# A hybrid network on one core: another order of the pieces on each engine, and another placing of the spare products

## The chip, the cores and the metric

The kernel runs on one core of one Trainium2 chip. A core has TensorE (PE in the profile), VectorE (DVE), ScalarE (ACT), GpSimd (POOL) and SyncE (SP), which issues DMAs. Each engine has its own stream of instructions and works through it in order; engines wait for each other through semaphores. The metric is device time of one execution in microseconds, lower is better.

## What is computed

2048 tokens of width 128 pass through eight residual stages. Each stage normalizes x and adds its result:

```python
x = x + _L0_attn_a_ref(_layernorm(x), ...)   # recurrence over the tokens, with clips
x = x + _L0_ffn_ref(_layernorm(x), ...)      # gated experts, two of eight
x = x + _L0_attn_b_ref(_layernorm(x), ...)   # picks 15 earlier tokens, small MLP, palette
x = x + _L0_ffn_ref(_layernorm(x), ...)
x = x + _L1_attn_a_ref(_layernorm(x), ...)   # linear attention, cumulative sums
x = x + _L1_ffn_ref(_layernorm(x), ...)
x = x + _L1_attn_b_ref(_layernorm(x), ...)   # attention with decay, a scan
x = x + _L1_ffn_ref(_layernorm(x), ...)
return x
```

The first is a chain over all tokens: `delta = clip(v_t - v_old)` needs the state that the token before left.

## The kernel before

The tokens are 16 tiles of 128. A tile goes through twelve stages, each with a letter: `f` front (norm, q, k, v), `g` gram, `s` scan (the recurrence), `o` out, `a` ffn2, `p` pal (logits, top 15), `m` mix (gathered rows, MLP, palette), `b` ffn4, `l` lin, `c` ffn6, `d` dec, `e` ffn8. Nearly every stage is causal, so tile i of a later stage needs only tiles up to i of the one ahead of it. While the scan works on tile 12, mix may work on tile 9 and ffn8 on tile 6.

Each engine's code of a stage is a generator that stops at a `yield` ahead of each piece. `ORDER` holds one string for each engine; a letter stands for the next piece of that stage. So the strings are the whole schedule: 2240 pieces on PE, 3856 on DVE, 1776 on ACT, 992 on POOL, 80 on SP. The function `fast` walks a string:

```python
for n, letter in enumerate(ORDER[engine]):
    before(n)
    next(runs[letter])
```

The scan takes 8 tokens as a block, 256 blocks in all. On DVE a block is four products (L949), four bounded scans (L957), a transpose (L929), a mask (L965) and an addition (L972). On PE it is two pieces of four small products each: L571 waits for the transpose on DVE, and L581 waits for the mask. L965 waits for L571 and L972 waits for L581. Every block therefore crosses between DVE and PE four times, and what stands ahead of L571 or L581 in PE's string is done before them. Gram (L557) prepares the coefficients. Lines of other stages that are named below: ffn2 and ffn4 L635 to L659, pal L671 to L687, mix L699 to L754, lin L765 to L784, ffn6 and ffn8 L795 to L826, dec L838 to L858; L529 is the transpose of every norm. The addition to x is L1165 on DVE for mix.

PE has four PSUM banks for all that is not scan state; `bank` gives them in turn, and waits until the last reader of the bank is done. `FILL` has a digit for each of PE's 2240 pieces: so many spare products stand ahead of the piece, in the bank that it takes. They write nothing that is read, and are there to keep PE at work:

```python
for _ in range(idle[0]):
    e.matmul(b[:, 0:512], identb[:, :], mup[:, 0:512], start=True, stop=True)
```

Of the kernel before, what the change touches and what calls it, by code (L numbers as in the profile page):

```python
# [92 lines left out]
def pieces(stage):  # L93

    for k, _ in enumerate(stage):
# [14 lines left out]
        "ssfffggfgsfsgssssfsssgsgsfsfssgsssssssgsssssssfssgsossosoosssofsgsfsososssasaasgssasaasasasassgspspsssspfssp"  # L110
        "ppopsgsosoosossfssfsgsososssaasasgssasaasasasassgsssmsmspsmfsmspsmmomgsmmmsosoomsospmssmppsmsmspspogsomsfsmm"
        "smmgsfssasaasssmmmmsmmamsaamsasasasmmsmsmsgpsomspfmsosomsososmgspssmmmpppmssmommmpogsmmssmsmssssmmmssmssssss"
        "sassgsaasofmsmsoomaasmmsaosasasaosmmmfsbgsbbspmsopmmmsbombbsmfbbbsmgsmpslslppppsmmmmsmmmmsagllslallslmmamlsl"
        "smsfgcasmcccccsmsamscscasmscasasaodfsdsmmmddsbmdbbommmsodpdddpmbobsbmombbbsmsmmsmlsmlsomsfspsmmmmmlllmslllop"
        "psppgmmfslflgmmscsgccccscsmcsmscssmasmcmsmsaaseseeeeemmmsdoseedasedddosoaooamddsmddasaasmmmsgsmmbmbsbmsopfmp"
        "osbmbmbsgbbsbmspgmspslppsmpmmmlsmamgasamllglllslmmsfamsaalmslfsamsascamcsccmmscccscbssbcbsopsepeeeeedsbseebd"
        "edddbsoombboddddsbosmmmmmsmmlsglssmmsmsomsllllllsommmsmsplslpsppmpmsamscfcmmmmmccccgasaccsmmcasmsaamedaseaem"
# [1944 lines left out]
```

## Time and profile before

| | us |
|---|---|
| median of three runs | 1591.43 |
| lowest and highest | 1584.05, 1592.32 |
| the profiled execution | 1597.4 |
| its span, first to last instruction | 1594.9 |
| PE busy (L517 of it) | 1352.4 (227.1) |
| DVE busy | 1066.4 |
| POOL busy | 906.0 |
| ACT busy | 843.5 |
| mean granted TensorE clock | 0.876 |

PE is the busiest engine, and a sixth of its busy time is spare products. A granted clock of 0.876 is a mean over stretches at 2.4 GHz and stretches at 1.2 GHz. Idle time of an engine costs something only where the chain that ends last passes through it.

### The profile page before, as it was taken

Reading aid. Unit: us, or ns where it says so; the run is one execution under the profiler, and the core shown is the slowest. Engines: PE = TensorE matmul, PEld = TensorE weight load, DVE = VectorE, ACT = ScalarE, POOL = GpSimd, SP = SyncE. Lnnn points to the kernel's source line nnn. Section 1 sums busy time; section 2 is a strip of 40 time slices with the busy share of each in tenths; the row PEclk is TensorE's granted clock in tenths of the full one; section 3 lists DMA queues with packets and bytes.
Section 4 is the critical chain, followed back from the end, with each engine's and each line's share of the span. In section 5 each row is a group of like instructions: output and inputs, shape, how many; then the busy total and the mean of one; then the engine's idle time right before and its main releaser. Section 6 shows DMA issues by size and latency. Waiting matters only on the chain.

```text
span 1594.9 us, 54156 instructions
## 1 busy us (share of the span) xinstructions
PE 1352.4 (85%) x21798; PEld 915.9 (57%) x21958; DVE 1066.4 (67%) x4616; ACT 843.5 (53%) x2254; POOL 906.0 (57%) x1527
## 2 busy tenths in 40 slices
PE   2668888888889898888899898899999899998886
PEld 1234555456567566656566565656666566765654
DVE  2787877878678867786866767586786746544332
ACT  1233254356475647474673746456464647565464
POOL 2545677567666847565766656465565456453331
PEclk8567668797989999988988899798899989999999
DMA  5000010000000101010100101000010101010000
GB/s 161 1 1 12 24 29 23 16 9 26 9 25 7 30 5 32 4 31 4 29 7 7 29 2 31 4 19 19 3 29 9 30 4 31 6 29 4 3 3 7
DMA packets 24294, 30.12 MB, mean 19 GB/s; under 512 B 9089, under 2 KB 18978, under 8 KB 24034
## 3 DMA queue, kind: packets, MB, share of 16 engines
q0 software_dynamic: 8304, 16.73, 4.1%
q1 hardware_dynamic: 15730, 9.82, 2.1%
q8 instruction: 176, 2.88, 0.8%
q14 instruction: 84, 0.69, 0.1%
HBM read 25.21 MB, written 2.29 MB: 17 GB/s over the span
## 4 chain that ended last, share of the span: by engine, by line
PE 54%; DVE 19%; ACT 11%; issue 8%; POOL 6%; SPq 1%; DMA 0%; DVEq 0%; ACTq 0%; POOLq 0%
PE ps L517 6%; PE ps L659 4%; PE ps L557 4%; DVE ps L957 4%; PE ps L754 3%; PE ps L712 3%; PE ps L742 2%; DVE ps L949 2%; PE ps L684 2%; PE ps L772 2%; PE ps L571 2%; POOL sb L1775 2%; PE ps L581 2%; PE ps L775 2%; PE ps L598 2%
## 5 line engine op out<-in xcount | busy, mean ns | idle before, releaser
L957 DVE TENSOR_TENSOR_SCAN ps<-ps,sb 128x47 f32<-128x47 f32 (+3 forms) x1024 | 272.0, 266 | 43.9 <-DVE ps L949 0.9
L1775 POOL DMA_INDIRECT sb<-table,sb x240 | 233.7, 974 | 92.9 <-issue 66.6
L517 PE MATMUL ps<-sb 128*128 128x512 bf16 x766 | 227.1, 396 | 17.1 <-issue 5.6
L949 DVE TENSOR_TENSOR ps<-sb,ps 128x24 f32<-128x24 f32 (+3 forms) x1024 | 192.9, 188 | 15.3
L517 PEld LDWEIGHTS ps<-sb 128*128 128x128 bf16 x926 | 86.5, 103 | 79.6 <-issue 20.9
L1639 POOL TENSOR_SCALAR sb<-sb 128x1 f32<-128x1 f32 x128 | 29.1, 227 | 170.5 <-DVE sb L892 164.6
L581 PEld LDWEIGHTS ps<-sb 32*32 32x32 f32 x2032 | 43.8, 112 | 123.3 <-issue 83.2
L571 PEld LDWEIGHTS ps<-sb 32*32 32x32 f32 x2032 | 43.6, 113 | 114.1 <-DVE sb L929 56.4
L898 DVE TENSOR_TENSOR sb<-ps,sb 128x128 f32<-128x128 f32 x112 | 31.8, 285 | 110.3 <-PE ps L826 57.8
L1289 ACT ACTIVATE sb<-sb 128x128 f32<-128x128 f32 x128 | 62.1, 489 | 81.6 <-POOL sb L1645 81.2
L571 PE MATMUL ps<-sb 32*32 32x32 f32 x2032 | 72.1, 214 | 36.4 <-DVE sb L929 33.8
L581 PE MATMUL ps<-sb 32*32 32x12 f32 x2032 | 66.1, 192 | 38.5 <-DVE sb L965 27.4
L557 PE MATMUL ps<-sb 128*128 128x480 f32 x128 | 85.7, 761 | 4.4 <-POOL sb L1678 2.3
L965 DVE TENSOR_TENSOR sb<-ps,sb 128x32 f32<-128x32 f32 x254 | 45.8, 180 | 57.8 <-PE ps L571 56.8
L1587 ACT ACTIVATE sb<-ps,sb 128x128 bf16<-128x128 f32 x256 | 71.1, 375 | 23.2 <-PE ps L816 23.0
L659 PE MATMUL ps<-sb 128*128 128x128 f32 x512 | 81.9, 312 | 0.0
L1678 POOL TENSOR_TENSOR sb<-sb 128x480 f32<-128x480 f32 x64 | 65.9, 1037 | 24.8 <-ACT sb L1333 24.7
L1643 POOL TENSOR_TENSOR sb<-sb 128x1 f32<-128x1 f32 x128 | 72.9, 569 | 10.8 <-POOL sb L1639 0.2
L972 DVE TENSOR_TENSOR ps<-sb,ps 128x12 f32<-128x12 f32 x254 | 41.0, 162 | 52.1 <-PE ps L581 51.0
L1817 POOL TENSOR_TENSOR sb<-sb 128x360 f32<-128x360 f32 (+1 forms) x48 | 48.7, 1017 | 46.2 <-ACT sb L1541 45.8
L1359 ACT ACTIVATE sb<-ps 128x480 f32<-128x480 f32 x64 | 37.0, 579 | 70.2 <-PE ps L557 68.7
L659 PEld LDWEIGHTS ps<-sb 128*128 128x128 f32 x512 | 73.6, 222 | 0.9
(310 smaller groups left out, 3777.0 us busy)
## 6 DMA issues: line engine op xcount, KB each, us to landing
sb<-table,sb POOLq DMA_INDIRECT x240
sb<-in_cs SPq DMA_DIRECT2D x16, 128.0 KB
table<-sb SPq DMA_DIRECT2D x17, 64.0 KB, 1.5
sb<-in_x SPq DMA_DIRECT2D x4, 256.0 KB, 8.0
sb<-dscr SPq DMA_DIRECT2D x64, 2.0 KB
out<-sb SPq DMA_DIRECT2D x16, 64.0 KB
sb<-in_mdn POOLq DMA_DIRECT2D x1, 512.0 KB, 9.9
sb<-in_wex SPq DMA_DIRECT2D x1, 512.0 KB, 7.4
```

The source lines that it names most:

```text
L517: e.matmul(b[:, 0:512], identb[:, :], mup[:, 0:512], start=True, stop=True)
L557: e.matmul(b[:, 0:32 * LW], blk, g_.pp[j % 2][:, :], start=True, stop=True).then_inc(*g_.P("s"))
L571: x = e.matmul(psS[rows, 0:32], KZT[c % 2][rows, 32 * o1:32 * o1 + 32], R[g % 2][rows, :], start=g == 0, stop=True, skip_group_check=True)
L581: x = e.matmul(b[rows, 0:12], SB[g % 2][rows, :], KM[c2 % 2][rows, 4 * o2:4 * o2 + 4, :].rearrange("p a b -> p (a b)"), start=True, stop=True)
L659: x = e.matmul(b[:, 0:128], s.hw[j // 4][:, 128 * (j % 4):128 * (j % 4) + 128], wex[:, 128 * j:128 * j + 128], start=False, stop=j == 7)
L949: e.tensor_tensor(at(psP, p + ROW - 3 - 2 * m, [ROW, 3], [2, m], [1, 2]), AC[:, row(n, k), :, HIST - 2 * m:HIST].rearrange("p r (a b) -> p ...
L957: e.tensor_tensor_scan(at(psD, 16 + k + COMB * skip, [COMB, 3 * ROW - skip]), at(psP, p + skip, [1, 3 * ROW - skip]), Q[:, i % 32, skip:3 ...
L1289: e.activation(s.xn[c % 2][:, :], X[:, s.tile(c), :], ACT.Identity, bias=st[:, 10:11], scale=st[:, 9:10]).then_inc(*s.A("xn"))
L1587: x = e.activation(s.w[:, 128 * at:128 * at + 128], bk.of[s.name, "d", g, c][:, 128 * j:128 * j + 128], ACT.Copy, scale=t[:, 40 + at:41 + at])
L1643: e.tensor_tensor(st[:, 9:10], st[:, 8:9], mhalf[:, 0:1], ALU.pow).then_inc(*s.G("lr"))
L1678: e.tensor_tensor(g_.pp[j % 2][:, :].rearrange("p (a b c) -> p a b c", b=2, c=LW), at(KT[c % 3], 32 * j, [2, 16], [0, 2], [1, LW]), km[:, ...
L1775: e.indirect_dma_start(GA[:, k, :], None, table[0:128 * i + 128, :] if i else table0, bass.IndirectOffsetOnAxis(u[:, k:k + 1], 0)).then_in ...
```

## The change

The five strings of `ORDER` are replaced and so is `FILL`; nothing else. Each engine has as many pieces of each stage as before, so no work of the network is added or taken away. By the digits in the code, the spare products are 1026 at 396 places, where they were 926 at 382. At the same place in the string another letter stands at 1658 of 2240 places on PE, 1350 of 3856 on DVE, 1240 of 1776 on ACT, 613 of 992 on POOL and 36 of 80 on SP. One line of PE's string and one of `FILL`:

```diff
-        "ppopsgsosoosossfssfsgsososssasaasgssasaasasasassgsssmsmspsmfsmspsmmomgsmmmsosoomsospmssmppsmsmspspogsomsfsmm"
+        "sppogsoossoossspsgssssososssasasasssasaasfasasasfgsmspsmspmsmsgospmfsmsosoopsompmmpmmmsmpmssmsgsmossosmmsmmf"
...
-    "0105000000010100000001010100000910002100000000100000000000100000010000010000000100100000000000000001000010000000"
+    "0010040007002403026034007010009021100200000101000400000000000200000130000000000000000006000100009000000107100000"
```

**Place 1: PE, about block 79 of 256 of the scan (the end of the scan's tile 4).** L571 and L581 are the scan's two pieces, L517 is a spare product. Before:

```order
L571 MATMUL ps<-sb 32x32 x4
L581 MATMUL ps<-sb 32x12 x4
L571 MATMUL ps<-sb 32x32 x4
L517 MATMUL ps<-sb 128x512 x3
L581 MATMUL ps<-sb 32x12 x4
L571 MATMUL ps<-sb 32x32 x4
L529 MATMUL ps<-sb 128x128
L517 MATMUL ps<-sb 128x512 x2
L581 MATMUL ps<-sb 32x12 x4
L571 MATMUL ps<-sb 32x32 x4
L517 MATMUL ps<-sb 128x512
```

Now:

```order
L571 MATMUL ps<-sb 32x32 x4
L635 MATMUL ps<-sb 128x8
L636 MATMUL ps<-sb 128x8
L640 MATMUL ps<-sb 128x128 x3
L641 MATMUL ps<-sb 128x128
L581 MATMUL ps<-sb 32x12 x4
L742 MATMUL ps<-sb 32x16 x80
L571 MATMUL ps<-sb 32x32 x4
L742 MATMUL ps<-sb 32x16 x16
L581 MATMUL ps<-sb 32x12 x4
L517 MATMUL ps<-sb 128x512 x2
L529 MATMUL ps<-sb 128x128
```

Where spare products alone stood between two steps of the scan, products of ffn2 and ffn4 (L640, L641) and of mix (L742) stand now. Over the whole of the scan's tile 4, PE has 104 pieces where it had 72.

**Place 2: PE, the end of mix for tile 11 (the last L754 of the tile).** Before:

```order
L754 MATMUL ps<-sb 32x128 x16
L614 MATMUL ps<-sb 128x128
L615 MATMUL ps<-sb 128x128
L571 MATMUL ps<-sb 32x32 x4
L754 MATMUL ps<-sb 32x128 x32
L529 MATMUL ps<-sb 128x128
L581 MATMUL ps<-sb 32x12 x4
L699 MATMUL ps<-sb 128x128 x4
L765 MATMUL ps<-sb 128x384
L571 MATMUL ps<-sb 32x32 x4
```

Now:

```order
L816 MATMUL ps<-sb 128x128
L815 MATMUL ps<-sb 128x128
L816 MATMUL ps<-sb 128x128
L754 MATMUL ps<-sb 32x128 x16
L815 MATMUL ps<-sb 128x128
L816 MATMUL ps<-sb 128x128
L815 MATMUL ps<-sb 128x128
L816 MATMUL ps<-sb 128x128
L815 MATMUL ps<-sb 128x128
```

The end of mix for tile 11 now stands 45 pieces nearer to the start of PE's string, and products of ffn6 and ffn8 (L815, L816) stand about it where steps of the scan and pieces of mix, pal and lin stood.

**Place 3: PE, behind the end of mix for tile 15, the last one.** L754 ends the tile's mix. Before:

```order
L754 MATMUL ps<-sb 32x128 x64
L772 MATMUL ps<-sb 128x360
L775 MATMUL ps<-sb 128x360
L858 MATMUL ps<-sb 128x128 x8
L772 MATMUL ps<-sb 128x360
L517 MATMUL ps<-sb 128x512
L529 MATMUL ps<-sb 128x128
L775 MATMUL ps<-sb 128x360
L635 MATMUL ps<-sb 128x8
```

Now:

```order
L754 MATMUL ps<-sb 32x128 x64
L529 MATMUL ps<-sb 128x128
L517 MATMUL ps<-sb 128x512 x2
L795 MATMUL ps<-sb 128x8
L798 MATMUL ps<-sb 128x128
L799 MATMUL ps<-sb 128x128
L807 MATMUL ps<-sb 128x128 x4
L517 MATMUL ps<-sb 128x512 x6
L529 MATMUL ps<-sb 128x128
```

Before, 92 pieces of PE stand behind that L754 and now 82; those of lin (L772, L775) and dec (L858) that followed it at once have gone ahead of it.

## Rows read from the trace of the kernel before

**Rows 1.** The page, part 1: busy time of each engine, share, instructions.

```profile
PE 1352.4 (85%) x21798; PEld 915.9 (57%) x21958; DVE 1066.4 (67%) x4616; ACT 843.5 (53%) x2254; POOL 906.0 (57%) x1527
```

**Rows 2.** The page, part 4: shares of the chain that ended last, by engine.

```profile
PE 54%; DVE 19%; ACT 11%; issue 8%; POOL 6%; SPq 1%; DMA 0%; DVEq 0%; ACTq 0%; POOLq 0%
PE ps L517 6%; PE ps L659 4%; PE ps L557 4%; DVE ps L957 4%; PE ps L754 3%; PE ps L712 3%; PE ps L742 2%; DVE ps L949 2%; PE ps L684 2%; PE ps L772 2%; PE ps L571 2%; POOL sb L1775 2%; PE ps L581 2%; PE ps L775 2%; PE ps L598 2%
```

**Rows 3.** Starts of L1165 (adds mix) and L957 (scan); the tile-11 L1165 in time order.

```profile
L1165 DVE SCALAR_TENSOR_TENSOR sb<-ps,sb x16: 319/349/352, 246.6 to 1499.3; 128x128 f32<-128x128 f32 x16
...
L957 DVE TENSOR_TENSOR_SCAN ps<-ps,sb x1024: 203/267/447, 45.0 to 1286.0; 128x47 f32<-128x47 f32 x86, 128x51 f32<-128x51 f32 x85
...
1220.03 0.35 DVE L1165 SCALAR_TENSOR_TENSOR sb<-ps,sb 128x128 f32<-128x128 f32 x1 [0.45 <-PE ps L754]
```

**Rows 4.** Stretches: PE, PEld, DVE, ACT, POOL busy (instructions), TensorE clock, DMA share, GB/s.

```profile
0.00:246.90 246.90, 167.38 (x2207) 95.44 (x2230) 170.38 (x883) 77.38 (x224) 129.87 (x253) 0.69 0.13 37
246.90:1220.40 973.50, 857.26 (x14652) 591.97 (x14754) 711.86 (x3154) 554.43 (x1477) 615.76 (x1026) 0.90 0.06 17
1220.40:1367.80 147.40, 134.84 (x2321) 94.99 (x2335) 94.32 (x324) 88.22 (x225) 79.00 (x117) 0.93 0.07 19
1367.80:1431.00 63.20, 59.17 (x1035) 41.03 (x1042) 29.94 (x75) 37.49 (x97) 31.94 (x49) 0.95 0.07 18
1431.00:1499.60 68.60, 58.87 (x1058) 43.58 (x1061) 27.17 (x71) 36.48 (x91) 25.34 (x39) 0.93 0.03 6
1499.60:1594.90 95.30, 74.87 (x532) 48.94 (x539) 32.70 (x112) 49.50 (x140) 24.12 (x46) 0.97 0.01 4
...
1306.50:1367.80 61.30, 57.53 (x1050) 42.16 (x1056) 33.94 (x91) 40.29 (x106) 36.85 (x55) 0.97 0.09 22
```

**Rows 5.** The same stretches, instructions of L517 (spare products) alone: PE, PEld.

```profile
0.00:246.90 246.90, 17.62 (x46) 6.73 (x68) 0.69 0.13 37
246.90:1220.40 973.50, 118.63 (x392) 45.35 (x495) 0.90 0.06 17
1220.40:1367.80 147.40, 26.61 (x97) 10.18 (x111) 0.93 0.07 19
1367.80:1431.00 63.20, 17.83 (x60) 6.78 (x67) 0.95 0.07 18
1431.00:1499.60 68.60, 12.12 (x41) 4.24 (x46) 0.93 0.03 6
1499.60:1594.90 95.30, 34.29 (x130) 13.26 (x139) 0.97 0.01 4
```

**Rows 6.** The page, part 5: groups of scan and gram on PE.

```profile
L571 PE MATMUL ps<-sb 32*32 32x32 f32 x2032 | 72.1, 214 | 36.4 <-DVE sb L929 33.8
L581 PE MATMUL ps<-sb 32*32 32x12 f32 x2032 | 66.1, 192 | 38.5 <-DVE sb L965 27.4
L557 PE MATMUL ps<-sb 128*128 128x480 f32 x128 | 85.7, 761 | 4.4 <-POOL sb L1678 2.3
```

**Rows 7.** Scan tile 4 and all behind the scan, each engine; then L517 there.

```profile
246.80:297.30 50.50, 38.70 (x701) 21.41 (x707) 38.48 (x207) 21.77 (x56) 36.40 (x53) 0.79 0.10 26
1286.00:1594.90 308.90, 269.91 (x4123) 190.09 (x4150) 134.91 (x375) 171.10 (x452) 129.60 (x206) 0.95 0.04 11
...
1286.00:1594.90 308.90, 76.71 (x278) 29.32 (x307) 0.95 0.04 11
```

**Rows 8.** Two stretches with their clock, then L659 on PE in each.

```profile
173.50:193.50 20.00, 17.40 (x211) 12.26 (x212) 15.77 (x86) 5.31 (x18) 10.27 (x18) 0.50 0.06 18
471.00:555.00 84.00, 76.26 (x1277) 52.83 (x1284) 67.33 (x302) 49.88 (x139) 56.88 (x97) 1.00 0.07 17
...
L659 PE MATMUL ps<-sb x12: 421/421/582, 175.8 to 178.8; 128*128 128x128 f32 x12
...
L659 PE MATMUL ps<-sb x32: 274/275/378, 501.2 to 533.6; 128*128 128x128 f32 x32
```

**Rows 9.** The last chain, from 1499 us on: its summary line.

```profile
by line: issue 22.2%; ACT sb L1575 4.6%; ACT sb L1579 4.5%; PE ps L517 4.0%; PE ps L850 3.2%; DVE sb L1223 3.1%; POOL sb L1643 3.0%; PE ps L775 2.7%; ACT sb L1587 2.3%; PE ps L772 2.1%; POOL sb L1842 2.0%; ACT sb L1289 2.0%; PE ps L659 1.9%
```

More of the change, by code:

```diff
@@ new lines @@
+        "smmsmmslsopslopspmmsmmgllllllsmmaspaammlglsmsmfmcmascpcccsmmmmaccsacsascsaasfseeeeesemsmmdemsesmdedsddbmbbmm"
+        "spdgdddmmmsbpombsboosbsbbososglfsslssmlllosllslommmspglspslmmmspmmammmascaccccpscpgmsccscmssmmsammedsmaemeee"
+        "sedefaedddsaaaesfdmmsdddsmmmmmpsmgsbmsbbsmmmosfbpsoosboogsbsmbbsbsmmmssolpslsmmmosppslllllslmamamammsppggsfl"
+        "mslmmmscfsmmmamcsccccsaassccaascsgsammmmmmesmmeeeeesdmmesmsmdesdbsddebbsoddsfdpdsobobboosbsbbpsgmmmlsmslomsm"
+        "mspmospplllmmmsmlllsappmsagasmllmsmfgmmsmmscfcccccsascscaascasaasseeeemmemsmesedesmpdmbmesddbpdbgmsgsdddsodm"
@@ new lines @@
+        "daaagsddsddasaaosmsmbsobbsooospmbmsbpbmmmsbbbsosmopmsmmmlpsplsmsmsallllllsmmasalsmmslmmppcsccccsccccsseeeeee"
+        "daeesmdsemsaddmmmmdmmasmddaaasdmsdmmsbmbbpmssommpobobmbmobbbompmmmmmlplmmoplllolllmmpplmmlaaammcccccccccaeaa"
+        "deedmeemmdmdmmmmdaaammeemmddeddbebbpmmpmmbbbmmmpbbbppmmmmbpblblmpmmllllllbbbmbbbmlmmlmmlclcccccllllccllcleld"
+        "eeedmmdeddemmmmemmeddeddmmmcmccmmmbmbbmmccmmmcmmmbcbbcmbbbcmmmldlmdmemmdddlleeleeldddeldlemmmmemmmmlelmmmmcc"
+        "ccbccbbcccbbbeeeebbbeedelldedddlllllleldldddcccccccccedeedededdeeeddeddeeeeeeeee",
@@ new lines @@
+    "POOL":
+        "ffffggfggggfffggggffgggggffggggoofgoooooooffggapggppppfpggoogppppooooooopppappppppfggppgpfgfppppfoopggfooooo"
+        "ppooppppappmmppppppmpfgfggpggfpppoogpoooooooggpagfpppppppppppmbmpppmppfgffggpglpppoollllollloooooocgpaggfgpp"
+        "ppppppdppppgpppddddmmgfmbpgffggoogggooofloopooplllpllpllapgggcgppppppppppedppppgmmpmddddbpgffooppfppoooooolo"
+        "ggpfllllalllppppcpppppppppmmppedmgpbgggfffddddgooppppolooooollollglglflagpggcpppppppppppdegppppmgmddmddpfbfg"
+        "fooppppfoooooologggpllllallplpppppcgpppppfgmmppppmedbgpggffddddoofoooolopppoopgllplllalglggpppppcpppmmpppppp"
+        "edmbpfpffgggddddoopppgpooooloogopllllalllggcpppppppmpmpepdppmppppbggfddddggppooppgooolfoooopllllallflfggcggp"
+        "pppppppppmmppedmpppbpfgggddddppppoooloooooolflllplallffgcgggfpppppppedppggppppmmppgmddddggbpoooooooooppplfpa"
+        "fpflllllllggggcgmmmedggppppppppppppdddpdppbooggpoooopopoopplpalllllllcmmmppedppppppppppddpddppbpooppppopoloo"
+        "ooolllllllacppppppmmpedmppppppddddbppppppppblllllllplpppppplcpmpllllppllmledmppppddddcbldellmmlddddlmlllcbed"
+        "lllllldlldddceddddde",
@@ L197 @@
     "SP":
[L198 removed]
+        "ppppmpppmpppmppmpppmppepppemppmpeeppmppmpppppeempmpppemeppppmpepmeppeppmppmeeeee",
 }
 FILL = (
[L201 to L203 removed]
```

186 lines of the change are left out of this document (82 added, 104 removed).

## The prediction, made before the changed kernel ran

> **What bounds the kernel now.** I read the busy times first. PE is busy for 1352.4 of 1594.9 us, DVE for 67%, the others for less [rows 1]. The chain that ended last lies on PE for 54% and on DVE for 19% [rows 2]. So no engine is full, and PE's stream is what most work queues in. Next I cut the execution where mix of a tile ends (L1165), because mix has the most work per tile; it ends first at 246.6 us, for tile 11 at 1220.4 and for tile 15 at 1499.6 [rows 3]. For each stretch I read PE's busy time [rows 4] and take off the spare products [rows 5]. The reader is to see three parts:
>
> - 0 to 246.9 us: PE has 167.4 - 17.6 = 149.8 us of real work and 79.5 us of idle time, at a granted clock of 0.69. The pipeline of tiles fills here.
> - 246.9 to 1220.4: 857.3 - 118.6 = 738.6 us of real work in 973.5 us, so 1.318 us pass for each us of real work. 116.2 us are idle. The clock is 0.90.
> - Behind it: 1220.4 to 1367.8 has 108.2 us of real work in 147.4 (a ratio of 1.362), the stretch to 1431.0 has 41.3 in 63.2, the one to 1499.6 has 46.8 in 68.6, and the last has 40.6 in 95.3. The scan is over at 1286.0 [rows 3].
>
> The last stretch is another kind: 22% of its chain is issue, and ACT, DVE and POOL lines follow each other in it [rows 9]. There the last tile's own path decides, not the amount of work on PE.
>
> **The change.** Nothing is added but 100 spare products, and the other pieces are the same in number. So the question is where PE's work stands relative to the things that end the stretches. I count letters of PE's two strings up to each end of a mix tile. The price of a piece comes from the trace: a scan piece costs (72.1 + 66.1) / 512 = 0.27 us, a gram piece 85.7 / 64 = 1.34 us [rows 6], and any other (1352.4 - 227.1 - 138.2 - 85.7) / 1664 = 0.54 us [rows 1, 5, 6]. A spare product costs 227.1 / 926 = 0.245 us of PE, the sums of the busy time and of the weight loads of L517 [rows 5].
>
> Step 1, up to the end of mix 11 (place 2): 45 pieces fewer, namely 10 of scan, 1 of gram and 34 others. That is -2.7 - 1.3 - 18.4 = -22.4 us of real work. By the ratio 1.318 it gives -29.5 us. DVE's string agrees in direction (that L1165 stands 85 pieces earlier), and so do ACT's (32) and POOL's (20), so I see no engine that would keep PE waiting for what has been drawn ahead.
>
> Step 2, mix 12 and 13: most of it comes back. Mix 12 has 7 scan pieces, 1 gram piece and 19 others more (+13.5 us), mix 13 has 3 scan pieces and 7 others more (+4.6 us). At 1.362 that is +24.7 us.
>
> Step 3, mix 14: 26 other pieces more, +14.1 us. The ratio would be 1.53 here, but 17.8 us of the stretch are spare products, and their number falls from 67 to 49. I therefore add up: 41.3 + 14.1 of work, 49 x 0.245 = 12.0 of spare products, 4.0 of idle time as before, 71.4 us. That is +8.2.
>
> Step 4, mix 15: 8 other pieces fewer (-4.3), spare products 18 for 47. The sum would be 42.5 + 4.4 + 9.7 = 56.6 us. The shortest distance between two ends of mix in the tail is 61.3 us (tile 13, from 1306.5 to 1367.8) [rows 4], and mix has its own path of gathered rows, MLP and palette, so I take 61.3: -7.3 us.
>
> Step 5, behind mix 15 (place 3): 10 pieces fewer (-5.4) and 101 spare products for 139 (-9.3). All of it on the path would be -14.7; none, 0. As the row of the last chain shows issue and other engines rather than PE, I take -5.
>
> Step 6, the spare products ahead of mix 11: 734 for 563. Of these, 64 more stand ahead of mix 0, where 79.5 us of PE are idle: they cost nothing there, and 15.7 us at most if that cover were gone. The other 107 come to 26.2 us beside 116.2 us of idle time. L517 has about 6% of the chain [rows 2], 94 us of its 227, or 0.41. By that share they cost 10.7 us; the ends are 0 and 26.2. Against it stands the clock. A 128x128 float32 product of L659 takes 421 ns where the granted clock is 0.50 (1.2 GHz) and 275 ns where it is 1.00 (2.4 GHz) [rows 8], 35% less. One hundredth more of granted clock over 973.5 us is 19.5 us less at 1.2 GHz; with 54% of the chain on PE that is 19.5 x 0.54 x 0.35 = 3.7 us. More spare products between the pieces may bring 0 to 0.06. I take 0.03, -11.1 us, and let the two cancel.
>
> The Trainium skill (TensorE: Matmul & The Clock Gate, section Terms) prices throttled time at the time times (1 - K/N), one half. By that the 0.03 would be 29 us and not 11, and the sum some 18 us lower. The trace speaks against it for this mix of work: the product above loses 35% and not 50%, and only part of the time has PE on the chain.
>
> **Place 1, the one that speaks against the change.** In the scan's tile 4 PE has 72 pieces and is busy for 38.7 of 50.5 us, at least 6 us of it spare products [rows 7]. It gets 32 pieces more: 2 front, 8 ffn2, 9 ffn4 and 14 mix, less 1 gram: 33 x 0.54 - 1.34 = +16.5 us. These come to about 49 us of real work in a stretch of 50.5, so L571 and L581 will be behind them and the scan must slow down here, by 10 to 20 us. What is queued behind it on DVE are the four products and scans of each block. I cost it at nothing more than step 1 counts, because later stages have a backlog of two tiles and get their work done in that time. It costs if the scan's end decides (below).
>
> **The sum:** -29.5 + 24.7 + 8.2 - 7.3 - 5 + 0 = -8.9 us. The profiled execution took 1597.4 us (its span is 1594.9), so it would be 1588.5. The median of the three runs is 1591.43, 0.99626 of the profiled one; by that the forecast is 1582.6 us.
>
> **Rivals.**
>
> *The spare products do not fit (slower).* On PE they run ahead of the piece for which they stand, and if that piece's inputs are there, everything behind it is late. Then the work moved ahead of mix 11 brings its bare 22.4 us and not 29.5, and the 107 cost their whole 26.2: +3.8 in place of -29.5, so +24.4 in all. 1621.8, or 1615.7 on the median's scale. It decides from about a third of the 107 on the path beyond the share taken. For it speaks that L517 is on the chain for more time than any other line [rows 2]; against it, the 116 us of idle time.
>
> *The scan's end decides (no change).* On PE the scan's last piece stands 23 pieces later: 14 mix, 6 dec, 2 ffn4, 1 pal, 12.5 us, x 1.318 = +16.4 us. What follows is the last tile's path, 308.9 us, of which PE is busy for 269.9 and 76.7 are spare products [rows 7]. If only the work that moved is saved there (12.5), the result is +3.9: 1601.3, or 1595.3. For it speaks place 1, and that this stretch has 210 spare products for 310 only because less idle time is there to fill; against it, that mix's backlog hides a late scan.
>
> *The clock (clearly faster).* The spare products fit, cost nothing, and raise the clock of the long stretch by 0.06: -22.2 beside -8.9. 1566.3, or 1560.4. For it: the clock is at 0.69 in the first stretch and 0.90 in the long one [rows 4], with 79.5 and 116.2 us of idle time to fill. Against it: in the first stretches DVE's scan sets the pace, which a faster PE helps little. By the skill's rule named above this case would be still lower; I have not used that.
>
> **Chances.** The forecast 0.40, the clock 0.24, spare products that don't fit 0.19, the scan's end 0.14, anything else 0.03. A measurement of this kernel can tell about 0.5%, 8 us, from no change. The forecast is just beyond that, so I split its 0.40 into 0.22 faster, 0.15 the same, 0.03 slower. The clock gives 0.24 faster; the spare products 0.19 slower; the scan's end 0.11 the same and 0.03 slower; the rest 0.01 the same and 0.02 slower. In sum 0.46 faster, 0.27 the same, 0.27 slower. The range reaches from the clock's case with a little more (1556) to the spare products' case (1618). The likeliest case alone, with the ends of steps 5 and 6, spans 1568 to 1603.
>
> **What would show it.** Step 1: the L1165 of tile 11 at about 1191 us and not 1220. Steps 2 and 3: mix 13 ends 5 us earlier than before (about 1363) and mix 14 some 3 us later (1434). Step 4: 61 us from mix 14 to mix 15. Step 5: about 90 us from there to the end. Step 6: a granted clock of about 0.93 in the long stretch, with L517 at about 0.4 of its busy time on the chain. Place 1: the scan's tile 4 takes 60 to 70 us and not 50, and the scan ends 10 to 20 us later than 1286. The forecast is wrong if mix 11 does not end earlier, or if idle time on PE in the long stretch stays near 116 us although the spare products are more.

## The result, and the profile after

The changed kernel takes 1546.18 us in the median of four runs (1541.74 to 1548.0), beside 1588.37 us for the kernel before on the same chips. The ratio is 0.972, with a 95% interval from 0.966 to 0.977. The forecast was 1582.6 us, with a range down to 1556: the sign was right, the size was missed by a factor of five, and the time lies below the range. The profiled execution took 1547.8 us where that of before took 1597.4, so 49.6 us have to be found in the traces; by the medians it is 42 us, because the profiled execution of before was slower than all the timed ones (1592.32 at most).

The page after: busy times, spare products, the chain that ended last by engine and by line.

```profile
PE 1360.1 (88%) x22058; PEld 893.6 (58%) x22058; DVE 1056.4 (68%) x4616; ACT 840.2 (54%) x2253; POOL 909.9 (59%) x1527
...
PE 60%; DVE 14%; ACT 8%; POOL 8%; issue 7%; SPq 1%; DMA 0%; DVEq 0%; POOLq 0%; ACTq 0%
PE ps L517 9%; PE ps L659 4%; PE ps L557 4%; PE ps L754 4%; PE ps L712 3%; PE ps L742 2%; DVE ps L957 2%; PE ps L571 2%; POOL sb L1775 2%; PE ps L581 2%; PE ps L598 2%; PE ps L684 2%; DVE sb L1223 2%; PE ps L772 2%; PE ps L601 2%
...
L517 PE MATMUL ps<-sb 128*128 128x512 bf16 x1026 | 304.2, 399 | 7.6 <-ACT sb L1575 1.7
```

Against [rows 1] and [rows 2]: PE is busy for 88% of the span and not 85%, and 60% of the chain lie on it and not 54%. L517 has 9% of the chain where it had 6%. So the spare products hold more of the path than in the page of before (which lacks some of them, see below), and the kernel is faster nonetheless. The granted clock is 0.914 for 0.876.

There is also a thing about [rows 1] that I had in front of me and did not use. There PE shows 21798 products to 21958 weight loads. After shows 22058 to 22058. The trace of before lacks 160 records, all of L517: 766 products in its page (a sum of 227.1 us) to the 926 weight loads of [rows 5]. A spare product is 304.2 / 1026 = 0.30 us of PE, and 227.1 / 766 is the same. My 0.245 divided the time of 766 by 926. The missing ones also read as idle time of PE: at the weight loads of the 103 that the long stretch lacks, the trace of before shows gaps of about 12 us in all, so I estimate the 116.2 us of idle time in the prediction at 104.

The same cuts as in [rows 4] and [rows 5], at the ends of mix 0, 11, 13, 14 and 15 (stretch; PE, PEld, DVE, ACT, POOL busy; clock; DMA), then L517 alone.

```profile
0.00:252.10 252.10, 177.26 (x2319) 96.27 (x2319) 174.35 (x900) 77.41 (x228) 132.46 (x258) 0.76 0.13 37
252.10:1160.80 908.70, 843.56 (x14620) 557.85 (x14621) 672.90 (x3034) 542.41 (x1439) 587.22 (x975) 0.94 0.06 17
1160.80:1329.40 168.60, 156.16 (x2524) 107.86 (x2522) 114.59 (x413) 94.26 (x246) 105.69 (x162) 0.96 0.08 20
1329.40:1408.30 78.90, 69.59 (x1135) 50.22 (x1134) 41.47 (x105) 46.00 (x124) 45.09 (x67) 0.98 0.08 20
1408.30:1461.90 53.60, 48.17 (x993) 37.20 (x992) 22.86 (x67) 32.42 (x82) 18.82 (x29) 0.88 0.01 4
1461.90:1546.00 84.10, 65.32 (x476) 44.21 (x474) 30.22 (x102) 47.69 (x136) 20.59 (x39) 0.93 0.02 4
...
0.00:252.10 252.10, 40.83 (x131) 11.50 (x131) 0.76 0.13 37
252.10:1160.80 908.70, 179.29 (x604) 53.66 (x604) 0.94 0.06 17
1160.80:1329.40 168.60, 35.98 (x124) 11.24 (x123) 0.96 0.08 20
1329.40:1408.30 78.90, 13.51 (x49) 4.39 (x49) 0.98 0.08 20
1408.30:1461.90 53.60, 5.68 (x19) 1.99 (x20) 0.88 0.01 4
1461.90:1546.00 84.10, 28.87 (x101) 9.27 (x99) 0.93 0.02 4
```

Beside [rows 4] the six stretches changed by +5.2, -64.8, +21.2, +15.7, -15.0 and -11.2 us. The pattern of the forecast is there: early at mix 11, given back up to mix 14, gained again behind it. Step 2 was foreseen within 4 us (+21.2 for +24.7); all others are larger than forecast. PE is idle for 65.1 us of the long stretch.

Start and end of mix's additions and of the scan, for [rows 3]; and the scan's tile 4 (place 1), for [rows 7].

```profile
L1165 DVE SCALAR_TENSOR_TENSOR sb<-ps,sb x16: 325/351/352, 251.8 to 1461.5; 128x128 f32<-128x128 f32 x16
...
L957 DVE TENSOR_TENSOR_SCAN ps<-ps,sb x1024: 200/267/445, 44.8 to 1261.9; 128x47 f32<-128x47 f32 x86, 128x51 f32<-128x51 f32 x85
...
247.70:311.30 63.60, 56.77 (x1247) 39.02 (x1243) 47.97 (x250) 30.30 (x79) 43.88 (x75) 0.89 0.08 22
```

The scan's tile 4 takes 63.6 us for 50.5, as its 32 further pieces on PE led me to expect. But the scan ends at 1261.9 and not later than 1286.0.

### The profile page after: what moved, and what is told of

Read it like the earlier page. It is cut to its first block, busy times and chain, and to the rows that moved or that the text cites. A ratio compares the mean times of both kernels' runs of the same rounds, so it can differ in the third digit from the quotient of the medians.

```text
span 1546.0 us, 54480 instructions
## 1 busy us (share of the span) xinstructions
PE 1360.1 (88%) x22058; PEld 893.6 (58%) x22058; DVE 1056.4 (68%) x4616; ACT 840.2 (54%) x2253; POOL 909.9 (59%) x1527
## 4 chain that ended last, share of the span: by engine, by line
PE 60%; DVE 14%; ACT 8%; POOL 8%; issue 7%; SPq 1%; DMA 0%; DVEq 0%; POOLq 0%; ACTq 0%
PE ps L517 9%; PE ps L659 4%; PE ps L557 4%; PE ps L754 4%; PE ps L712 3%; PE ps L742 2%; DVE ps L957 2%; PE ps L571 2%; POOL sb L1775 2%; PE ps L581 2%; PE ps L598 2%; PE ps L684 2%; DVE sb L1223 2%; PE ps L772 2%; PE ps L601 2%
## 5 line engine op out<-in xcount | busy, mean ns | idle before, releaser
L517 PE MATMUL ps<-sb 128*128 128x512 bf16 x1026 | 304.2, 399 | 7.6 <-ACT sb L1575 1.7
L957 DVE TENSOR_TENSOR_SCAN ps<-ps,sb 128x47 f32<-128x47 f32 (+3 forms) x1024 | 272.1, 266 | 42.7
L517 PEld LDWEIGHTS ps<-sb 128*128 128x128 bf16 x1026 | 92.1, 102 | 87.6 <-issue 23.1
L581 PEld LDWEIGHTS ps<-sb 32*32 32x32 f32 x2032 | 42.2, 109 | 104.8 <-issue 69.3
L571 PEld LDWEIGHTS ps<-sb 32*32 32x32 f32 x2032 | 42.0, 109 | 100.8 <-DVE sb L929 48.8
L571 PE MATMUL ps<-sb 32*32 32x32 f32 x2032 | 70.0, 209 | 24.3 <-DVE sb L929 23.8
L557 PE MATMUL ps<-sb 128*128 128x480 f32 x128 | 81.1, 726 | 2.9 <-POOL sb L1678 2.4
L581 PE MATMUL ps<-sb 32*32 32x12 f32 x2032 | 64.8, 189 | 18.1 <-DVE sb L965 13.4
L1643 POOL TENSOR_TENSOR sb<-sb 128x1 f32<-128x1 f32 x128 | 72.6, 568 | 10.7 <-POOL sb L1639 0.2
L659 PE MATMUL ps<-sb 128*128 128x128 f32 x512 | 76.1, 299 | 0.0
L754 PE MATMUL ps<-sb 16*32 16x128 f32 x2048 | 71.4, 290 | 0.0
L659 PEld LDWEIGHTS ps<-sb 128*128 128x128 f32 x512 | 68.9, 210 | 2.2 <-issue 1.4
```

The source lines that it names most:

```text
L557: e.matmul(b[:, 0:32 * LW], blk, g_.pp[j % 2][:, :], start=True, stop=True).then_inc(*g_.P("s"))
L571: x = e.matmul(psS[rows, 0:32], KZT[c % 2][rows, 32 * o1:32 * o1 + 32], R[g % 2][rows, :], start=g == 0, stop=True, skip_group_check=True)
L581: x = e.matmul(b[rows, 0:12], SB[g % 2][rows, :], KM[c2 % 2][rows, 4 * o2:4 * o2 + 4, :].rearrange("p a b -> p (a b)"), start=True, stop=True)
L659: x = e.matmul(b[:, 0:128], s.hw[j // 4][:, 128 * (j % 4):128 * (j % 4) + 128], wex[:, 128 * j:128 * j + 128], start=False, stop=j == 7)
L754: x = e.matmul(b[32 * q:32 * q + 32, 0:128], WT[rows, k:512:16], palW[rows, 128 * k:128 * k + 128], start=k == 0, stop=k == 15)
L957: e.tensor_tensor_scan(at(psD, 16 + k + COMB * skip, [COMB, 3 * ROW - skip]), at(psP, p + skip, [1, 3 * ROW - skip]), Q[:, i % 32, skip:3 ...
```

## The experiments

All ratios are to the kernel before, timed on the same chip in turn with it. Intervals are 95%.

| kernel | order | spare products | ratio | interval | clock in the profile |
|---|---|---|---|---|---|
| before | before | 926 | 1 | | 0.876 |
| after | after | 1026 | 0.972 | 0.966 to 0.977 | 0.914 |
| bo_none | before | 0 | 1.015 | 1.006 to 1.025 | 0.783 |
| ao_none | after | 0 | 1.001 | 0.997 to 1.006 | 0.791 |
| bo_afill | before | after's 1026, by piece | 1.051 | 1.042 to 1.061 | 0.883 |
| ao_bfill | after | before's 926, by piece | 1.030 | 1.021 to 1.040 | 0.876 |
| spB_11_none | before, after's behind mix 11 | 0 | 1.004 | 1.000 to 1.008 | 0.785 |
| spA_12_none | after, before's behind mix 12 | 0 | 1.012 | 1.006 to 1.018 | 0.786 |
| af_front | after | 734 ahead of mix 11's end | 0.979 | 0.972 to 0.987 | 0.891 |
| af_back | after | 292 behind it | 0.991 | 0.987 to 0.995 | 0.818 |
| bf_front | before | 563 ahead of it | 1.007 | 1.003 to 1.011 | 0.801 |
| bf_back | before | 363 behind it | 0.994 | 0.991 to 0.997 | 0.787 |
| after_b | after | 1026 | 0.972 | 0.968 to 0.976 | 0.924 |
| af_gap_b | after | 603, placed by a trace | 0.978 | 0.973 to 0.984 | 0.874 |
| af_trim_b | after | 435 of 1026 | 0.986 | 0.983 to 0.990 | 0.851 |
| bf_gap | before | 614, placed by a trace | 0.980 | 0.975 to 0.985 | 0.884 |
| af_more | after | 1282 | 0.970 | 0.964 to 0.976 | 0.951 |
| af_gap2 | after | 692, two turns | 0.967 | 0.962 to 0.972 | 0.901 |

In the last column is the clock of one execution. A ratio compares a kernel with before on one chip; the kernels ran on five chips, in the groups bo_none to ao_bfill; the two spliced ones (spB, spA) with af_front and af_back; bf_front and bf_back; after_b to bf_gap; af_more and af_gap2. So a ratio of one group beside one of another carries the uncertainty of both.

af_trim and af_gap ran first on the chip of bf_front and bf_back, on which before took 1748 us, 10% more than elsewhere (0.976 and 0.967 there, clocks 0.809 and 0.829). On another chip the same two kernels came to 0.986 and 0.978, 1.0 and 1.2 points higher. bf_front and bf_back ran only on the slow chip, and a ratio from there can be off by as much.

### Order and spare products apart

My theory: the order makes the gain, and the spare products cancel. The rival: the spare products and the clock make it. Four kernels part them. Two have no spare products (the old lines are cut short here):

```diff
 FILL = (
-    "0000...",
+    "0" * 2240)
```

> The order of before with no spare products at all. It gives the base for the order alone, and says what the 926 spare products of before bring. If the order of the pieces makes the gain, the order of after without spare products is 2 to 3% faster than this kernel. If the spare products (the clock) make it, the two are within 0.5% of each other. For this kernel by itself: the granted clock falls from 0.88 to about 0.75, and the time rises by 2 to 5% over before, unless the 926 cost on PE what they give back in clock, when it is within 1%.

> The order of after with no spare products. Order theory: 0.97 to 0.98 of the order of before without spare products. Clock theory: 0.995 to 1.005 of it, at nearly the same clock of about 0.75.

Two have the other kernel's spare products, carried to the same pieces. One line of FILL, of bo_afill against before and of ao_bfill against after:

```diff
-    "1000010000100000000000000000100200000000100003000000000500000020000200100200000000000000010003000000000000000000"
+    "2200000000010000000000600000010000200000003020000001000000093000120000000000000010000210200000012000010000000000"
```

```diff
-    "0022040026000100000000000010000000020000000000010000000009301003000200000000001001200000100000200000200000000001"
+    "0010000000000000010000001501002000000010000000300000001200000000200000020000000000000100000000000000000000000000"
```

> The order of before, with the spare products of after: each of the 396 places goes with its piece (the k-th piece of its stage), so 1026 spare products stand ahead of the same pieces as in after. Clock theory (it is number and kind of place that count): 0.975 to 0.985 of before, at a clock of about 0.91. Order theory: 0.995 to 1.005 of before. A third theory, that spare products fit only the order for which they were placed, gives 1.005 to 1.02.

> The order of after, with the 926 spare products of before carried to the same pieces. Order theory: 0.97 to 0.98 of before. Clock theory: 0.995 to 1.005 of before, at a clock of about 0.88. The third theory (spare products fit only their own order): between the two, 0.98 to 1.0, with more L517 on the chain than after's 9%.

Measured: 1.015 and 1.001 without any, 1.051 and 1.030 with the other's. Without spare products the order is worth 1.001 / 1.015, or 1.4%. That is between the two theories (2 to 3%, and under 0.5%), so neither holds alone. The forecast had 0.55%. For bo_none by itself I had expected a clock of about 0.75 and 2 to 5% more time; it is 0.783 and 1.5%. The spare products bring 1.5% to before and 3.0% to after, from 1.001 to 0.972; so half of the result is theirs. At the other order's pieces some thousand of them cost 2.9% and 3.6% against none at all, although the clock (0.876 and 0.883) is far above the 0.78 without any. Of the three theories in the expectations the third, that they fit only the order for which they were placed, is nearest for both, and both came out slower than even it expected (1.051 for 1.005 to 1.02, 1.030 for 0.98 to 1.0). So neither their number nor the clock that they keep up decides, but where they stand. A count fits with this: in the traces without spare products, 377 of before's own 926 and 429 of after's own 1026 stand at a piece ahead of which PE is idle for over 0.1 us (41% and 42%); of those carried over it is 254 of 1026 in bo_afill (25%) and 187 of 926 in ao_bfill (20%). The first rival of the forecast was this mechanism, and it is real; only the change itself did not suffer from it.

The stretches of bo_none and then of ao_none, cut at the ends of mix 0, 11, 13, 14 and 15:

```profile
0.00:246.90 246.90, 157.66 (x2162) 92.55 (x2163) 170.95 (x887) 77.37 (x224) 130.66 (x254) 0.66 0.14 37
246.90:1230.60 983.70, 831.88 (x14260) 593.83 (x14258) 709.66 (x3148) 554.55 (x1477) 614.07 (x1024) 0.81 0.06 16
1230.60:1374.30 143.70, 121.34 (x2223) 89.95 (x2223) 94.84 (x325) 87.36 (x225) 79.11 (x117) 0.85 0.08 19
1374.30:1437.40 63.10, 54.65 (x975) 40.34 (x975) 29.79 (x77) 37.31 (x97) 31.94 (x49) 0.80 0.07 18
1437.40:1508.90 71.50, 58.70 (x1017) 45.42 (x1015) 27.20 (x71) 36.38 (x91) 25.52 (x40) 0.80 0.02 6
1508.90:1612.90 104.00, 65.31 (x403) 51.79 (x401) 32.89 (x112) 50.27 (x140) 23.91 (x45) 0.69 0.01 3
...
0.00:250.90 250.90, 154.96 (x2188) 91.80 (x2188) 175.79 (x900) 77.35 (x228) 132.26 (x258) 0.66 0.13 37
250.90:1175.60 924.70, 800.87 (x14014) 566.57 (x14014) 668.48 (x3034) 541.98 (x1439) 589.97 (x977) 0.82 0.06 17
1175.60:1351.30 175.70, 145.70 (x2402) 110.33 (x2401) 114.58 (x413) 95.02 (x246) 103.50 (x160) 0.83 0.07 19
1351.30:1434.70 83.40, 69.29 (x1086) 53.30 (x1086) 41.28 (x106) 46.32 (x124) 45.03 (x67) 0.82 0.07 19
1434.70:1486.60 51.90, 44.66 (x974) 35.47 (x973) 22.77 (x67) 32.14 (x82) 18.79 (x29) 0.89 0.02 4
1486.60:1576.90 90.30, 58.30 (x375) 48.63 (x375) 30.17 (x103) 48.59 (x136) 20.56 (x39) 0.67 0.01 4
```

The order alone changes them by +4.0, -59.0, +32.0, +20.3, -19.6 and -13.7 us, together -36.0. By the medians it is -24 (1614.5 and 1590.5): the profiled execution of ao_none was 12 us faster than its median, so single stretches here are good to some us only. The real work on PE up to the end of mix 11 falls from 157.7 + 831.9 = 989.6 us to 155.0 + 800.9 = 955.9. That is -33.7 for the 45 pieces, at nearly the same clock in both, and the forecast had -22.4.

### Where in the order the gain is

I believed that the gain is made by mix 11. Two kernels cut the strings in two, on all five engines, and carry on in the other's order. Of PE's string, spB_11_none against before, the line with the seam:

```diff
-        "mebddbbdooosodddsdbmpbmbmpmbbbsmsomosmmlsmlsmmspmsllsllsllspppspmmlsmmmlmmmasaammcmccscccmssccmmmmscsasaasee"
+        "mebddbbdooosodddsdbmpbmbmpmbbbsmsomosmmmmmmmmmsssmpmsmmmlpsplsmsmsallllllsmmasalsmmslmmppcsccccsccccsseeeeee"
```

> No spare products. All engines follow the order of before up to the end of mix 11 (PE's first 1767 pieces and what they need on the others), and then the order of after for what is left. If the order's gain is made ahead of mix 11 and partly given back behind it (in the two kernels without spare products the end of mix 11 was at 1230.6 and 1175.6 us and what followed took 382 and 401 us), this kernel has neither and is slower than both: about 1632 us in the profile. If the gain lies in the tail's order, it is at about 1590.

The line of spA_12_none with its seam, against after:

```diff
-        "daeesmdsemsaddmmmmdmmasmddaaasdmsdmmsbmbbpmssommpobobmbmobbbompmmmmmlplmmoplllolllmmpplmmlaaammcccccccccaeaa"
+        "daeesmdsemsaddmmmmdmmasmddaaasdmsdmmbsssbbpoooboobbbbbplolommmmllllllpmmmppppmmmmalmalammmcmccccmmmmccccaaaa"
```

> No spare products. All engines follow the order of after up to the end of mix 12, and then the order of before for what is left. By the same sum, after's way to mix 12 (1275.7 us) and before's behind it (302.6 us): about 1578 us in the profile, as the order of after itself (1576.9). If the gain lies in the tail's order, 1595 or more.

Measured: before's order with after's tail is at 1.004, just 0.3 points from after's order (1.001) and 1.1 from its own (1.015). After's order with before's tail is at 1.012. Both pairs say that the tail is worth 1.1 of the 1.4 points and the long front about 0.3. The front's part is smaller than the intervals and may be nothing; spliced and unspliced kernels ran on different chips, but the two ways to the tail's 1.1 agree. For the first my expectation of about 1632 us (1603 in its profile) was wrong by nearly 30 us, and for the second that of 1578 by 21; the alternative that I had named for each, that the gain lies in the tail's order, came closer. After's order ends mix 12 at 1277.3 us in spA_12_none, 33 us ahead of bo_none (1310.4), and with before's tail 13 us of that are left at the end of the span (1599.5 to 1612.9). Even these come from one fast execution: by the medians spA_12_none is 0.3 points ahead of bo_none. Pieces that are put off until after a milestone make the milestone earlier and are paid behind it; its earlier date is no gain.

Behind the end of mix 15 the part of the tail can be seen by itself. The last stretch of bo_none and ao_none stands above, with 104.0 and 90.4 us. That of spB_11_none (after's tail) and then of spA_12_none (before's tail):

```profile
1511.00:1601.40 90.40, 58.68 (x375) 48.49 (x375) 29.96 (x103) 48.74 (x136) 20.58 (x39) 0.67 0.01 4
...
1495.50:1599.50 104.00, 65.02 (x403) 51.67 (x401) 32.93 (x112) 50.34 (x140) 24.13 (x45) 0.69 0.01 3
```

90.4 and 104.0: in these four traces it goes with the tail's order. On PE 375 products stand there in after's tail and 403 in before's. Step 5 of the forecast had this part with the value -5, of which the 10 pieces could give -5.4 at most (the rest of its bound of -14.7 was spare products); here, without any spare products, it is -13.6.

### Where the spare products gain

Two kernels have a part of after's spare products each. af_front keeps those ahead of the end of mix 11, af_back those behind. One line of FILL, of the part that is set to zero in each:

```diff
-    "3000020100000000000000010002300609049100100000000000000000000000000000000000000001200000000000000000000003010000"
+    "0000000000000000000000000000000000000000000000000000000000000000000000000000000000000000000000000000000000000000"
```

```diff
-    "0022040026000100000000000010000000020000000000010000000009301003000200000000001001200000100000200000200000000001"
+    "0000000000000000000000000000000000000000000000000000000000000000000000000000000000000000000000000000000000000000"
```

> The order of after with its own spare products, but those behind the end of mix 11 left out (734 of 1026 stay). The spare products of after bring 2.8% over the same order without any. If the long stretches ahead of mix 11 carry that (idle time there and a clock of 0.82 without them), this kernel keeps three quarters of it: about 0.979 to 0.984 of before.

> The order of after with only the 292 spare products behind the end of mix 11. If the gain goes by the share of the time, this one keeps a quarter: 0.990 to 0.997 of before. If the tail, where the last tile's own path decides, gains most from the clock (0.67 in the last 90 us without spare products), it keeps half or more, 0.98 to 0.988.

The same for the order of before:

```diff
-    "0000000000000010402170000551000013200307000000000004000000000000030000000001011000000010000000000000030000000000"
+    "0000000000000000000000000000000000000000000000000000000000000000000000000000000000000000000000000000000000000000"
```

```diff
-    "1000010000100000000000000000100200000000100003000000000500000020000200100200000000000000010003000000000000000000"
+    "0000000000000000000000000000000000000000000000000000000000000000000000000000000000000000000000000000000000000000"
```

> The order of before with its 563 spare products ahead of the end of mix 11, and none behind it. All 926 bring 1.5% here. Ahead of mix 11, after's 734 brought 2.2 points. If it is the front where after's placing is the better one, this kernel is at 1.005 to 1.015 of before (it keeps 0 to 1 point of the 1.5). If it is the back, it keeps 1.5 or more: 0.99 to 1.0.

> The order of before with only its 363 spare products behind the end of mix 11. If the front's are the poor ones, this keeps 1 point or more of the 1.5: 0.998 to 1.006 of before. If the back's are, 1.01 to 1.02.

In after, the 734 of the front bring 1.9 points (0.991 to 0.972) and the 292 of the tail 0.7 (0.979 to 0.972). Alone, without the others, they bring 2.2 and 1.0 (from 1.001). In before the 363 of the tail bring as much, 0.7 (1.007 to 1). But the 563 of the front cost 0.6: without them before is at 0.994. That is where I had expected the poor ones, though bf_back, at 0.994, lies below both ranges that I gave for it. So my reading was that before's spare products did harm in the front.

That is not shown. The last two numbers come from the slow chip, where the two kernels that were timed elsewhere too had ratios lower by 1.0 and 1.2 points, more than the 0.6 in question. And the traces from the other chips show no harm: mix 11 ends at 1220.4 us with before's spare products and at 1230.6 without any (after: 1160.8 and 1175.6), while on the slow chip it ends at 1363.8 with the 563 (bf_front) and at 1343.2 without them (bf_back). What is shown is the whole, 1.5% for before's and 3.0% for after's.

### Are spare products free where the trace shows PE idle?

For the count above I matched PE's instructions in the traces without spare products to the pieces of the string, and took the idle time ahead of each piece. Ahead of mix 11's end 192 of before's 563 spare products stand at a place with over 0.1 us of it, and 280 of after's 734; behind it 185 of 363 and 149 of 292. The tails are alike in this too, half and half; in the front 34% and 38% are too close to explain the difference by this count alone. af_trim keeps 435 of after's spare products, those at a place with over 0.1 us of idle time in that trace or with some left behind them in after's own. af_gap drops all places and takes new ones: at each piece that takes a bank and has over 0.3 us of idle time ahead of it, as many as fit at 0.25 us. Lines of FILL against after:

```diff
-    "0022040026000100000000000010000000020000000000010000000009301003000200000000001001200000100000200000200000000001"
+    "0000040026000000000000000010000000000000000000000000000000000003000000000000000000000000000000000000200000000000"
```

```diff
-    "0022040026000100000000000010000000020000000000010000000009301003000200000000001001200000100000200000200000000001"
+    "0000012012200000000000000030000000000000000000000500000000070002000000000000000000000040000000000000000000000000"
```

> The order of after, with 435 of its 1026 spare products: those at places where the trace of the order without spare products shows PE idle for over 0.1 us before the piece, or where the trace of after shows idle time left behind them. If a spare product is free only in a gap that the trace shows, the 591 that are left out only cost, and this is faster than after: 0.955 to 0.968 of before. If they pay through the clock wherever they stand, it loses some of it: 0.980 to 0.990.

> The order of after, with 603 spare products at 204 new places: wherever the trace of this order without spare products shows PE idle for over 0.3 us before a piece that takes a bank, as many as fit at 0.25 us each. If gaps in one trace say where spare products are free, this is as good as after or better: 0.960 to 0.975 of before. If the gaps of one execution aren't where those of the next are, it costs: 0.99 to 1.02, as the carried ones did.

On the slow chip: 0.976 and 0.967. So that they could be set beside after, both ran again on one chip with it, and with the same rule on the order of before:

```diff
-    "1000010000100000000000000000100200000000100003000000000500000020000200100200000000000000010003000000000000000000"
+    "0000010000000000000000000001000100000000000000000002000000000210000000000200000000000000000005001000000000000000"
```

> The changed kernel again, on one chip with the three below, so that they can be compared with it directly: 0.965 to 0.977 of before.

> The order of after with 603 spare products at the 204 places where the trace without spare products shows PE idle for over 0.3 us. In the last comparison it was at 0.967 of before, on a chip on which every kernel took 10% longer. If that holds here it equals after (0.965 to 0.977) with 423 spare products fewer, and number and clock don't matter as much as place. If it came from that chip's longer idle times, 0.98 to 0.99 here.

> 435 of after's spare products, those at places with idle time. 0.976 of before in the last comparison. If the 591 left out are neither cost nor gain: as after. If they pay through the clock: 0.5 to 1 point slower than after.

> The order of before with spare products placed by the same rule as in af_gap, from the trace of its own order without any. If before's own 926 are placed poorly and the rule is good, this takes the order of before to 0.980 to 0.990 of before, and what is left to after is the order's own 1.4 points. If before's order has less room for spare products wherever they stand, it is 0.995 or more.

Measured: 0.972, 0.978, 0.986 and 0.980. af_gap_b falls just behind the range for "equals after" (0.965 to 0.977), and af_trim_b lost 1.4 points where I had expected 0.5 to 1. The last is the one that tells most. The order of before, with 614 spare products at other places in place of 926, is 2.0% faster than before. Its clock; from its page the lines on busy time and chain, the chain's lines and its spare products; and its long stretch:

```profile
core 0: 1568.6 us, clock 0.884
...
PE 1337.2 (85%) x21646; PEld 880.1 (56%) x21646; DVE 1063.7 (68%) x4616; ACT 842.1 (54%) x2254; POOL 908.0 (58%) x1527
...
PE 49%; DVE 22%; ACT 12%; issue 8%; POOL 7%; SPq 1%; DMA 0%; DVEq 0%; ACTq 0%; POOLq 0%
DVE ps L957 4%; PE ps L517 4%; PE ps L754 4%; PE ps L659 4%; PE ps L557 3%; PE ps L712 3%; DVE ps L949 3%; POOL sb L1775 3%; PE ps L684 2%; PE ps L742 2%; PE ps L772 2%; PE ps L571 2%; PE ps L775 2%; PE ps L581 2%; PE ps L850 1%
...
L517 PE MATMUL ps<-sb 128*128 128x512 bf16 x614 | 193.9, 430 | 51.7 <-DVE ps L972 8.2
...
247.10:1204.50 957.40, 838.42 (x14557) 565.31 (x14556) 709.79 (x3154) 554.44 (x1477) 615.50 (x1025) 0.90 0.06 17
```

The clock is 0.884, and before had 0.878 to 0.889 on that chip: the same. L517 has 4% of the chain for 6%. The end of mix 11 is at 1204.5 us, 16 earlier than in [rows 4], with the same 0.90 of clock in the long stretch. So another placing, with a third fewer spare products, gives the 2.0% at an equal clock. Fewer at the old places was not tried in this order; in after's (af_trim_b) it cost time. With spare products placed by the same rule the two orders are at 0.978 and 0.980, alike within their intervals: the 1.4 points that the order has without spare products are not seen any more.

But the trace of the order without spare products does not say it all. The 591 that af_trim drops stand where that trace shows no gap of 0.1 us, and they are worth 1.4 points (0.986 to 0.972). Two things could make it: with the spare products in, PE waits elsewhere than in that trace; or they pay through the clock (0.851 in af_trim_b, 0.924 in after_b). These runs don't part the two.

### More of them, and a better version

af_more adds 256 to after's, where two traces of after still show idle time. af_gap2 applies the rule a second time, on the trace of af_gap_b, and adds 89.

```diff
-    "0022040026000100000000000010000000020000000000010000000009301003000200000000001001200000100000200000200000000001"
+    "0022040026000100000000000040000000020000000000010600000009301003000200000000001001200040100000200000200000000001"
```

```diff
-    "0022040026000100000000000010000000020000000000010000000009301003000200000000001001200000100000200000200000000001"
+    "0000012012200000000000000050000000000000000000000500000000070002000000000000000000050040000000000000000000000000"
```

> After with 256 spare products more (1282), put where two traces of after both still show PE idle for over 0.3 us before a piece that takes a bank. If what is free can be read from the idle time, it is faster than after: 0.960 to 0.970 of before, at a clock of 0.93. If the little that is left is eaten by spare products that hold up PE, it is 0.972 to 0.985.

> The order of after with the spare products placed by its trace without any (603), and 89 more where the trace of that kernel still shows idle time over 0.3 us. A second turn of the rule: 0.970 to 0.978 of before if each turn finds free places, as af_gap (0.978) if it doesn't.

Measured: 0.970 and 0.967. Page lines of af_more, then of af_gap2 (clock; chain by engine; spare products):

```profile
core 0: 1542.0 us, clock 0.951
...
PE 59%; DVE 15%; ACT 10%; POOL 7%; issue 7%; SPq 1%; DMA 0%; DVEq 0%; POOLq 0%; ACTq 0%
...
L517 PE MATMUL ps<-sb 128*128 128x512 bf16 x1282 | 372.3, 395 | 27.0 <-DVE sb L1165 4.8
```

```profile
core 0: 1532.3 us, clock 0.901
...
PE 45%; DVE 18%; ACT 12%; POOL 12%; issue 10%; SPq 1%; DMA 0%; DVEq 0%; POOLq 0%; ACTq 0%
...
L517 PE MATMUL ps<-sb 128*128 128x512 bf16 x692 | 220.7, 432 | 45.5 <-DVE sb L1165 5.3
```

I expected 0.960 to 0.970 for af_more and 0.970 to 0.978 for af_gap2. af_more has the highest clock of all, 0.951, and 59% of its chain on PE; it is not clearly faster than after. af_gap2 has 692 spare products, a clock of 0.901 and 45% of the chain on PE, and it is the fastest kernel of the study, at 1543.3 us to 1598.6 for before on its chip. Its interval (0.962 to 0.972) and after's (0.966 to 0.977) overlap, so with two thirds of the spare products it is as good as after as far as these runs tell; that it is better is likely and not shown. Whether the order of before would get there too after a second turn was not tried.

## Why the prediction was wrong, point by point

**Which step failed.** Step 6 put the spare products at nothing, and they are half of the result; beside it steps 4 and 5 had the tail too small. The forecast for all up to the end of mix 14 was +3.4 us (steps 1 to 3, with 0 for step 6). The traces show -22.7 from before to after, and -2.7 between the two orders without spare products. So the moving of work was nearly the exchange that the forecast said, and the missing 20 us came in with the spare products. (These are single executions, and the one of ao_none was 12 us faster than its median.) For the two stretches behind mix 14 the forecast was -12.3 us; the traces show -26.2, and -33.3 without spare products.

**What bounds the kernel.** That no engine is full, that the fill, the long stretch and the tail have different limits, and that the last stretch hangs on the last tile's own path: no run speaks against it.

**Step 1** (end of mix 11 about 29 us earlier): it is 60 us earlier, 1160.8 for 1220.4, and 55 without spare products. The mechanism was right and the price too low. The 0.54 us for a piece came from PE's busy time less all of L517's. L517's time overlaps that of the products next to it, and taking it off took real work with it: in the trace of before the products other than L517 keep PE busy for 1192.1 us, not 1125.3. In bo_none, where none stand and the clock is lower, it is 1289.5 us. The earlier date was given back in steps 2 and 3, and the spliced orders show the same: the work is only moved. The forecast had that; my expectation of 1632 us for the first of them left it out.

**Steps 2 and 3** (+24.7 and +8.2, together +32.9): +36.9 in after, +52.3 without spare products. Right in kind; step 3 was low (+15.7 for +8.2).

**Step 4** (-7.3): -15.0. The shortest distance of two mix ends, 61.3 us, was taken for a floor. It is none: here it is 53.6 us, and 51.9 without spare products. A smallest value among four is no bound.

**Step 5** (-5, bounds 0 and -14.7): -11.2 in after, -13.7 and -13.6 in the two comparisons without spare products. I had allowed the 10 pieces -5.4 at most; the path got shorter by more than twice that. PE's busy time there fell by 7.0 us (65.3 to 58.3), and what the rest is was not looked into. This is the part of the order's gain that the experiments pin down best.

**Step 6** (0) is the step that failed, and it is half of the result. I let 10.7 us of cost and 11.1 us of clock cancel for *more* spare products. The question was not the 100 more but where all 1026 stand. The runs showed that all of before's bring 1.5% and all of after's 3.0%, so the new ones are worth 1.5 points more in their order than the old ones in theirs, some 24 us. bf_gap gains 2.0% in the order of before by another placing, at the clock of before. The forecast had no term for how well before's were placed. The clock of the long stretch rose from 0.90 to 0.94, between the forecast's 0.93 and the third rival's 0.96; by the 3.7 us for a hundredth it would give 15 us. The cost was too low in turn: at 0.30 us each, the 107 are 32 us and not 26.2. L517 was to be on the chain for 0.4 of its busy time; it is 9% of 1546.0 us, 139 of 304, or 0.46.

**The clock's price.** A granted clock of 0.876 is 24.8% of 1594.9 us at 1.2 GHz, and 0.914 is 17.2% of 1546.0: 130 us less. All that was gained is 49.6 us, by the ratios half of it the order's, and af_more, with 0.951, gained no more. The Trainium skill (TensorE: Matmul & The Clock Gate, section Terms) prices throttled time at the time times one half, which would be 65 us. The runs don't agree with it as a price of the whole time in this kernel; what the spare products cost in PE's time is in the measured number too and was not measured apart.

**The rivals.** The clock's case was nearest, at 1560.4, and still short by 14 us. Spare products that don't fit: the mechanism is real (2.9 and 3.6% when carried to the other order), and the change doesn't have it. The scan's end: tile 4 slowed as said, 63.6 us, and then the scan ended 24 us earlier; PE was no longer held up as often elsewhere. That last is argued, not shown.

**The range.** Its lower end was the clock's case with a little more, and it had no room for a gain by place. The narrower span of 1568 to 1603 mixes two scales: its lower end is in time of the profiled execution, and on the median's scale it is 1562.

**What stays open:** how the order's 1.4 points vanish once both orders have spare products placed by the same rule, whether the changed order as such is needed for 0.967, and in which stretches before's spare products stood badly.

## What to carry to other kernels

A milestone that comes earlier because work was moved behind it is not yet a gain; splice the two orders at the milestone and see what the end says. When instructions exist only to keep a clock up, ask of each whether its engine waits at that very place, and read it from a trace: 614 at places read from one beat 926 by 2%. And check that a trace has all records of a line (here products against weight loads) before dividing its time by a count.

## What the runs showed of the hardware that was not expected

One chip of the five on which the experiments ran took longer: 10% for before, 9% for af_gap and af_trim, the other kernels that ran there and elsewhere. The same kernel (af_gap and af_gap_b), the groups of two lines with very many small products, on the slow chip and then on another:

```profile
L742 PE MATMUL ps<-sb 15*32 15x16 f32 x4096 | 62.6, 191 | 34.9 <-issue 34.6 <-POOL sb L1794 0.3
L734 PE MATMUL ps<-sb 128*32 128x3 f32 x1920 | 49.2, 204 | 32.8 <-issue 31.5 <-ACT sb L1496 1.1
```

```profile
L742 PE MATMUL ps<-sb 15*32 15x16 f32 x4096 | 52.8, 187 | 17.7 <-issue 16.2 <-POOL sb L1794 1.4
L734 PE MATMUL ps<-sb 128*32 128x3 f32 x1920 | 37.6, 204 | 2.6 <-issue 1.5 <-ACT sb L1496 1.1
```

The mean product is as long on both (191 and 187 ns, 204 and 204), but PE stands idle ahead of L734 for 32.8 us and not 2.6, with no wait that the profile shows for most of it, and the span is 1707.6 us for 1559.6. L734's busy time is longer too (49.2 for 37.6 us), although each product is not, so they follow one another with less overlap. Busy and idle time of the two lines together make 69 of the 148 us; the clock is lower as well, 0.829 for 0.874. What makes the small products follow more slowly, and where the rest of the time goes, was not looked into.

The granted clock and the time do not go together across these kernels: a clock of 0.951 went with a ratio of 0.970, 0.901 with 0.967, and 0.883 with 1.051.
